# Last layer norm by halves, the last image placed by one-hot matmuls, bias rows spread by TensorE, row stores issued before weight fetches

## The reference, cut to what matters

```
h = tokenizer(x)                          # 8 images, 1024 tokens each, 256 wide
h = h + attention_layer(layernorm(h))     # 8 heads of 32
xf = layernorm(h)                         # "norm 3" of the kernel
H = gelu(xf @ W1 + b1)                    # 1024 wide
probs = softmax(H @ Wg + bg); assign = argmax(probs)      # 8 experts
y[token] = probs[token, assign] * (H[token] @ Wd[assign] + bd[assign])
out = h + y
```

## Time and profile before

| | |
|---|---|
| three runs | 1769.88, 1770.01, 1778.05 us, median 1770.01 |
| the profiled execution | 1766.45 us; its span from first to last instruction 1764.5 us |
| mean granted TensorE clock | 0.971 of full speed |
| busy share of the span | PE 91%, DVE 67%, ACT 53%, POOL 21% |
| last score of image 7 ends (PE) | 1403.96 us |
| first gather of rows is issued | 1483.89 us |
| second tile's turns begin; from here PE does a tile in 3.75 us | 1491.80 us |

### The profile page before, as it was taken

One profiled execution on the slowest core, in us unless ns is written; L12 is line 12 of the kernel. 1 busy time (PEld: TensorE's weight loads), 2 busy tenths in 40 slices (PEclk: granted clock), 3 DMA queues, 4 the chain that ended last, 5 costly groups with the idle time before them and its releaser, 6 DMA issues.

```text
span 1764.5 us, 29438 instructions
## 1 busy us (share of the span) xinstructions
PE 1610.8 (91%) x10934; PEld 1102.2 (62%) x10934; DVE 1185.5 (67%) x2070; ACT 940.5 (53%) x1564; POOL 369.2 (21%) x290
## 2 busy tenths in 40 slices
PE   8696999999999999999999999999888774999998
PEld 6463566555656565666466646664544363999998
DVE  2377777768686768677767776777765654555655
ACT  0364756665575657565756575658564751222222
POOL 0202000201120112012001301120110282555554
PEclk9898999999999999999999999999998986999999
DMA  4313044423533362436143604370429336566664
GB/s 172 88 47 81 13 120 96 109 50 92 118 77 84 65 139 49 111 49 135 42 114 55 154 15 114 58 164 2 96 61 215 72 85 163 189 211 212 212 201 143
DMA packets 131014, 188.57 MB, mean 107 GB/s; under 512 B 21606, under 2 KB 95980, under 8 KB 130620
## 3 DMA queue, kind: packets, MB, share of 16 engines
q1 hardware_dynamic: 112588, 121.57, 31.4%
q0 software_dynamic: 17856, 63.80, 11.2%
q10 hardware_dynamic: 432, 1.31, 0.2%
HBM read 85.55 MB, written 51.68 MB: 78 GB/s over the span
## 4 chain that ended last, share of the span: by engine, by line
PE 69%; DVE 11%; issue 8%; DMA 6%; ACT 4%; SPq 1%; POOL 1%; POOLq 0%; ACTq 0%; DVEq 0%
PE ps L576 12%; PE ps L827 12%; PE ps L590 11%; PE ps L543 8%; DVE nmax L1252 6%; PE ps L815 4%; PE ps L627 3%; PE ps L603 3%; PE ps L564 3%; ACT pr L953 3%; PE ps L610 3%; PE ps L649 3%; PE ps L651 2%; PE ps L650 2%; DMA xt<-x_in 2%
## 5 line engine op out<-in xcount | busy, mean ns | idle before, releaser
L1252 DVE TENSOR_REDUCE nmax<-ps 128x1 f32<-128x1024 f32 x512 | 623.6, 1221 | 220.9 <-PE ps L576 215.0
L953 ACT ACTIVATE pr<-ps,nmax 128x1024 f32<-128x1024 f32 x512 | 570.5, 1114 | 301.1 <-DVE nmax L1252 282.0
L576 PE MATMUL ps<-st 96*128 96x512 f32 x1024 | 400.5, 475 | 73.6 <-ACT pr L953 64.5
L576 PEld LDWEIGHTS ps<-st 96*128 96x128 f32 x1024 | 168.6, 192 | 270.7 <-ACT pr L953 133.4
L590 PE MATMUL ps<-pr,vs 128*32 128x256 f32 x4096 | 273.0, 387 | 10.9 <-DVE vs L1051 10.5
L827 PE MATMUL ps<-wd_high,hg 128*128 x1136 | 221.9, 288 | 0.0
L590 PEld LDWEIGHTS ps<-pr,vs 128*32 128x32 f32 x4096 | 109.3, 109 | 154.1 <-issue 73.7
L981 ACT ACTIVATE hg<-ps 128x512 fp32r<-128x512 f32 x142 | 77.4, 596 | 211.1 <-PE ps L815 211.1
L827 PEld LDWEIGHTS ps<-wd_high,hg 128*128 128x128 f32 x1136 | 182.1, 192 | 0.0
L543 PE MATMUL ps<-wp,xt 128*128 128x256 f32 x672 | 173.4, 379 | 3.4 <-DMA xt<-x_in 3.4
L827 PE MATMUL ps<-wd_low,hg 128*128 x568 | 160.8, 283 | 0.0
(11 more groups left out here) (153 smaller groups left out, 1938.8 us busy)
## 6 DMA issues: line engine op xcount, KB each, us to landing
st<-qk SPq DMA_DIRECT2D x192, 256.0 KB, 5.1
xt<-x_in SPq DMA_DIRECT2D x58, 384.0 KB, 4.1
token_rows<-staged_b SPq DMA_DIRECT2D x64, 256.0 KB, 4.9
token_rows<-staged_a SPq DMA_DIRECT2D x64, 256.0 KB, 4.9
token_rows<-hres POOLq DMA_DIRECT2D x8, 1024.0 KB, 5.4
wd_low<-w_down SPq DMA_DIRECT2D x64, 128.0 KB, 4.3
pr<-x_in SPq DMA_DIRECT2D x6, 384.0 KB, 10.0
rows<-token_rows,slot_from POOLq DMA_INDIRECT x71, 4.8
```

What stands on the lines that cost most here:

```text
L576: last = mm(ps[:, 2 * (k % SR) + j, :], stq[:, hh, i * P:(i + 1) * P], stk[:, hh, j * 512:(j + 1) * 512], start=True, stop=True)
L953: actv(pr[:, k % PR, :], ps[:, 2 * (k % SR):2 * (k % SR) + 2, :].rearrange("p a n -> p (a n)"), ACT.Exp, bias=nmax[:, k % 16:k % 16 + 1], ...
L1252: V.reduce_max(nmax[:, k % 16:k % 16 + 1], ps[:, 2 * (k % SR):2 * (k % SR) + 2, :].rearrange("p a n -> p (a n)"), AX_X, negate=True).then_ ...
```

## The change

1. SP: in image 7 the four `store_hidden` of image 6 are issued first, then `col`, then the weight pieces 0 to 14.
2. Norm 3 of the last image is done by halves on DVE and POOL (two `root_3`), and PE, ACT and DVE turn and split the first half alone; PE starts the hidden layer on it, and turns the second half after hidden chunk 2. POOL does 4 instead of 6 `split_down` before the first `root_3`.
3. The first half of the last image is no longer scattered: it is made one-hot like the second. Its 4 POOL scatters go, and 4 more one-hot matmuls (8 PE instructions as the profile counts them) come. `prefix` of the first half moves from after chunk 5 to after chunk 7; part of its `row_hot` is made between the copy and the sum of the logits; operations 8 and 9 of `route` (they give `prob`, which SP stores) move ahead of the count. POOL fetches `tab` before it waits for the stores of hidden rows.
4. `bd`, the bias row of each expert on all 128 partitions, was one broadcast DMA of 1 MB; now SP fetches 8 KB (`bd_raw`) in the place of `col`, ACT makes a selection matrix (`pick_row`), PE spreads the rows by 8 matmuls into four banks, and ACT copies them out.
5. The slots' experts (`slot_f`, `slot_expert`) are computed after `slot_from` and `slot_to`.

```diff
 (SP)
                 if before:
                     for u in range(4):
                         store_hidden(b - 1, u)
-                        if not after:
-                            for m in range(2 * u, 2 * u + 2):
-                                load_down(m)
                     if not after:
-                        for m in range(8, WD_PIECES - 1):
+                        sp.wait_ge(S["emb_mm"], IMAGES * TILES)
+                        sp.dma_start(col, column).then_inc(S["col_in"], 16)
+                        for m in range(WD_PIECES - 1):
                             load_down(m)
...
             sp.wait_ge(S["lg_done"], 2 * IMAGES)
-            sp.dma_start(col, column).then_inc(S["col_in"], 16)
+            sp.dma_start(bd_raw, b_down).then_inc(S["bd_raw_in"], 16)
             store_prob(IMAGES - 1)
-            sp.wait_ge(S["ff_mm"], 16 * IMAGES)
-            sp.dma_start(bd[:], b_down[None, :, :].broadcast_to([P, EXPERTS, D])).then_inc(S["bd_in"], 16)
...
 (POOL)
-            for m in range(6):
+            for m in range(4):
                 split_down(m)
-            root_3(IMAGES - 1)
+            for hf in range(2):
+                root_3(IMAGES - 1 + hf, slice(4 * hf, 4 * hf + 4))
+
+            pool.wait_ge(wd_in[2], 2 * 16 * (P // BLK))
             store_rear(IMAGES - 1, (IMAGES - 1) % 2)
             pool.wait_ge(S["xn_ready"], 2 * IMAGES)
-            for m in range(6, WD_PIECES):
+            for m in range(4, WD_PIECES):
                 split_down(m)
-            place(IMAGES - 1, IMAGES - 1, range(TILES // 2), IMAGES * STEPS - 4 * TILES)
             pool.wait_ge(S["row_ready"], 1)
             pool.wait_ge(S["lg_done"], 2 * IMAGES)
+            pool.wait_ge(S["table_out"], 16 * (ALL_TILES - TILES))
+            nc.gpsimd.indirect_dma_start(tab, None, table, bass.IndirectOffsetOnAxis(row_i[0:SLOTS, 0:1], 0)
+                                         ).then_inc(S["tab_in"], 16)
             for i in range(STAGED):
                 pool.wait_ge(row_out[i], 16 * IMAGES * 8)
-            pool.wait_ge(S["table_out"], 16 * (ALL_TILES - TILES // 2))
-            nc.gpsimd.indirect_dma_start(tab, None, table, bass.IndirectOffsetOnAxis(row_i[0:SLOTS, 0:1], 0)
-                                         ).then_inc(S["tab_in"], 16)
...
 (PE, router and end)
                     if k == 0:
-                        wait(pe, "xt_read", b * 4 + 4)
+                        wait(pe, "xt_read", b * 4 + (4 if b < IMAGES - 1 else 2))
                     if k >= 2:
                         wait(pe, "ff_act", b * 16 + k - 1)
                     hidden(b, 0, k, k)
+                    if b == IMAGES - 1 and k == 2:
+                        norm_turn(b, IMAGES * STEPS, (1,))
                 partial_logits(b, 0, 0)
+                wait(pe, "xt_read", b * 4 + 4)
...
-                    if b == IMAGES - 1 and k == HALF_PREFIX:
+                    if b == IMAGES - 1 and k == HC - 1:
                         prefix(b, ps[:, 0, :])
...
             prefix(IMAGES, ps[:, 1, :])
+            pe.wait_ge(S["bd_raw_in"], 16)
+            pe.wait_ge(S["sel_ready"], 1)
+            for e in range(EXPERTS):
+                last = mm(ps[:, 4 + e // 2, (e % 2) * D:(e % 2 + 1) * D], pick_row[:, e, :], bd_raw, start=True, stop=True,
+                          skip_group_check=True)
+                if e % 2 == 1:
+                    last.then_inc(S["bd_mm"], 1)
             pe.wait_ge(S["tab_in"], 16)
             mm(ps[:, 2, 0:SLOTS], tab, ident[0:SLOTS, 0:SLOTS], start=True, stop=False)
             pe.wait_ge(S["hot_ready"], 1)
-            for t in range(TILES // 2):
-                last = mm(ps[:, 2, 0:SLOTS], row_hot[:, t, :], slot_hot[:, t, :], start=False, stop=(t == TILES // 2 - 1))
+            for t in range(TILES):
+                last = mm(ps[:, 2, 0:SLOTS], row_hot[:, t, :], slot_hot[:, t, :], start=False, stop=(t == TILES - 1))
             last.then_inc(S["tab_mm"], 1)
+            pe.wait_ge(S["bd_in"], EXPERTS // 2)
...
 (ACT)
+            act.wait_ge(S["lg_done"], 2 * IMAGES)
+            actv(pick_row, ident[0:EXPERTS, 0:EXPERTS, None].broadcast_to([EXPERTS, EXPERTS, P]), ACT.Identity
+                 ).then_inc(S["sel_ready"], 1)
+            for i in range(EXPERTS // 2):
+                act.wait_ge(S["bd_mm"], i + 1)
+                actv(bd[:, 2 * i:2 * i + 2, :].rearrange("p e d -> p (e d)"), ps[:, 4 + i, :], ACT.Identity).then_inc(S["bd_in"], 1)
...
 (DVE)
+            def hot_rows(hf):
+                linked()
+                dve.wait_ge(S["col_in"], 16)
+                for t in range(4 * hf, 4 * hf + 4):
+                    at_tile = ALL_TILES - TILES + t
+                    last = V.tensor_scalar(row_hot[:, t, :], col, place_f[:, 0, t:t + 1], tid[:, at_tile:at_tile + 1],
+                                           ALU.is_equal, ALU.mult)
+                link(last)
...
                 logit_sums(last_b, hf)
+                if hf == 1:
+                    hot_rows(0)
                 keep_logits(last_b, hf)
...
-            for i in (0, 1, 2, 3, 4, 5, 6, 10):
+            for i in (0, 1, 2, 3, 4, 5, 6, 8, 9, 10):
                 route(last + 1, i)
```

More of the change, by code:

```diff
@@ L161, in vit_layer_kernel @@
         lt = xt_flat[:, 0:HALF]
+        row_hot = xt_flat[:, HALF:HALF + TILES * P].rearrange("p (t n) -> p t n", t=TILES)
+        col = row_hot[:, TILES - 1, :]
         staged = (staged_b, staged_a)
@@ L183, in vit_layer_kernel @@
         row_i = tensor(sc, "row_i", [P, 1], I32)
[L184 to L188 removed]
+        bd_raw = rows[0:EXPERTS, RING - 2, TILES * SLOTS:TILES * SLOTS + D]
+        pick_row = rows[0:EXPERTS, RING - 1, P:P + EXPERTS * P].rearrange("e (f n) -> e f n", f=EXPERTS)
+        slot_hot = rows[:, RING - 2, 0:TILES * SLOTS].rearrange("p (t n) -> p t n", t=TILES)
         sc.close()
@@ L442, in image @@
                 if before:
-                    root_3(b - 1)
+                    root_3(b - 1, slice(0, TILES))
                 if before:
@@ L629, in final, with norm_turn @@
                     last.then_inc(S["fin_mm"], 1)
-            def norm_turn(b, exps):
-                for j in range(4):
+            def norm_turn(b, exps, halves=(0, 1)):
+                for j in range(2 * halves[0], 2 * halves[-1] + 2):
                     hf, c = j // 2, j % 2
@@ L1004, in stats, with aggregate @@
                 aggregate(b, ln)
-            def aggregate(b, ln):
+            def aggregate(b, ln, tiles=range(TILES)):
                 hold(dve, f"stats{ln}", b + 1)
-                for t in range(TILES):
+                for t in tiles:
                     last = V.bn_aggr(mv[:, ln - 1, t, :], bst[:, ln - 1, t, :])
@@ L1088, in norm_3, with low_norm @@
                     last.then_inc(S["xn_ready"], 1)
-            def low_norm(b):
-                for j in range(4):
+            def low_norm(b, pieces):
+                for j in pieces:
                     piece = slice((j // 2) * HALF, (j // 2 + 1) * HALF)
@@ L1277, in _ @@
             added(last_b, last_par)
-            for t in range(TILES):
-                norm_3(last_b, last_par, t)
-            low_norm(last_b)
+            for hf in range(2):
+                for t in range(4 * hf, 4 * hf + 4):
+                    norm_3(last_b, last_par, t)
+                if hf == 0:
+                    low_norm(last_b, (0, 1))
             for hf in range(2):
@@ L1327, in _ @@
             linked()
-            link(V.tensor_tensor(pos[:, half], pos[:, half], cnt[:, 6, None, :].broadcast_to(each), ALU.add))
+            for hf in range(2):
+                link(V.tensor_tensor(pos[:, 4 * hf:4 * hf + 4], oh_half[:, (last + hf) % 2, GUARD:GUARD + TILES // 2, :],
+                                     cnt[:, 6, None, :].broadcast_to(each), ALU.mult))
             linked()
-            link(V.tensor_tensor(pos[:, half], pos[:, half], oh_half[:, IMAGES % 2, GUARD:GUARD + TILES // 2, :], ALU.mult))
+            link(V.reduce_sum(addr_f[:], pos[:], AX_X))
```

99 lines of the change are left out of this document (51 added, 48 removed).

## The result

| | before | after |
|---|---|---|
| median of 4 runs on one chip | 1771.13 us (1769.88 to 1778.05) | 1760.20 us (1757.43 to 1763.22) |
| ratio, with its 95% interval | | 0.993 [0.9907, 0.9953] |
| profiled execution (its span) | 1766.45 (1764.5) | 1760.89 (1759.1) |

The medians are 10.9 us apart. The same two kernels on another chip, later: 1767.92 (13 runs) and 1758.90 (8), ratio 0.995 [0.9932, 0.9967], 9.0 us. The forecast was 13.0.

What follows compares the result with a forecast made beforehand. PE, busy 91%, was taken to bound the kernel, with gains only where it waits: image 7's stores and the tail. 5.3 + 8.2 - 0.5 = 13.0 us off 1766.45 gives 1753.5, or 1757.0 against the runs' median; range 1752 to 1766.

Steps and rivals of the forecast that it cites:

- the likeliest case: Whole kernel: the forecast itself, 13.0 us off, 1757.0 against the runs' median; chance 72%.
- Part 1: Image 7, hidden-row stores issued before weights: ACT's third exponential 5.3 us sooner, bounds 3.7 to 5.3.
- Rival (b): Image 7: the earlier stores give nothing, leaving 7.7 us gained, 1762.3; chance 9%.
- Part 2: Last image's norm by halves: first half's hidden layer starts 4.2 us sooner, net 2.3 after turns and clock.
- -0.9 for the turns, -1.0 for the clock: Last hidden layer: losses set against the 4.2 us, for 8 turns moved between hidden chunks and for full speed returning differently.
- Part 3a: Tail: first prefix moved into PE's wait for the last Gelu, net 0.65 us gained.
- Part 3b: Tail without scatters: POOL fetches `tab` straight after `row_ready`, so it is there at 1470.6 instead of 1480.8.
- same moment: Tail: `hot_ready` from DVE at 1470.6, just when `tab` is there.
- Part 4: Tail, bias rows: `bd_raw` lands at 1466, matmuls end 1472.1, first gather at 1475.7, 8.2 us sooner.
- the slow bound: Tail: the 8 bias matmuls wholly at half clock, 7.2 us; 3.6 at full clock, 6.1 taken.
- Rival (a): Tail: `bd_raw` lands like `column`, 12.0 us after issue, so the tail gains nothing; 4.4 us off, 1765.6; chance 15%.
- Rival (c): Last hidden layer: PE stays at half clock, 19 us lost against 13 gained, 1776; chance 4%.

Runs made afterwards that it cites:

- part 1 alone: Kernel before with all 15 weight pieces issued behind the four hidden-row stores: 1761.66 us, ratio 0.9959 (second chip); 1761.00 us, 0.9960 (third chip).
- the norm in one piece: Changed kernel with the last norm whole again, four weight splits ahead of it kept: 1761.74 us, ratio 0.9965 (second chip); 1760.33 us, 0.9954 (third chip).
- the second trace: Trace of the changed kernel, nothing altered, run again on the third chip: 1758.90 us (8 runs), ratio 0.9950 to the kernel before.
- b_split_4: Kernel before with 4 instead of 6 POOL weight splits ahead of the norm, two more behind it: 1770.67 us, ratio 1.0015.
- the kernel of 1754.85 us: Changed kernel with fifth split before the norm, later routing, bias matmuls halved around the table, slots' experts ahead of the `tab_mm` wait: 1754.85 us, 0.9930.

## Why the prediction was right, and where not

The time was as forecast within 3.2 us and inside the range, and the likeliest case is the one that came. Its steps fared differently, and the total is nearer than they are. On the third chip part 1 alone gave 6.9 us for 5.3, and all the rest 2.1 for 7.7. That most of the forecast gain came all the same is in part luck.

**Part 1, right.** 5.4 us for 5.3, shown by undoing it and by doing it alone. What was not in it is the clock behind the stall, at half in the first 6 us in all three traces that have the stall. From the third exponential to the final projection the two first traces differ by 0.9 us, the trace where part 1 was undone by 8.9; how much of either is the stall's was not measured. Rival (b) did not occur: ACT's wait before the third exponential is 1.02 us, for DVE.

**Part 2, the start right, the net too large.** The first hidden matmul came 5.3 us sooner for 4.2 (turns at full clock, 1.12 us; POOL's power 1.05 for 1.67). The term "-0.9 for the turns, -1.0 for the clock" was mis-sized. What the runs showed in place of the net 2.3 is 0.8 us against the norm in one piece, by the trace, and 1.4 by medians that don't tell the two apart. The missing piece is a sentence of the prediction: that POOL's splits end later "and nobody needs them before 1480". Nobody needs their result, but DVE needs to run beside them. Its small operations with both inputs in SBUF were held until a split ended, 1.96, 2.44 and 1.82 us for 0.19, 0.18 and 0.15. This delayed `run`, PE waited for it, and the last logits ran at half clock. Whether DVE gets in between two splits or not matters little: the last held operation ended with the last split in either case (1452.43 and 1452.39 here, 1446.70 and 1446.65 in the second trace). That the hold goes with the splits is shown in both directions: two pieces more behind the norm brought it into the kernel before, and two less took one hold and 2.3 us away. The last logits' clock goes with the wait for `run`. Ten traces have the changed tail; in the five where PE waited 1.48 to 2.43 us for `run` the last logits took 2.81 to 3.47 us, in the five where it waited 0.85 us or not at all they took 1.92. So the price of the holds in the changed kernel's first trace is about 3.3 us, 1.77 of wait and 1.5 of clock.

The Trainium skill has the rule, in "SBUF — State Buffer", section "Who interferes with whom": a VectorE instruction with two inputs in SBUF contends with a GpSimd instruction that reads SBUF, and the one that was first blocks the other for its whole length. The traces agree, 12 splits of 2.355 us and holds that end on their ends. They show more than the rule says, too. DVE did not always get in when a split had ended: it stood through two ends in two traces (6.55 us each) and through one in two others (2.73 us in `b_split_4`, 3.19 with the norm in one piece). And the norm, whose operations have one tensor as input, was slowed beside a split (1.88 and 2.66 us for 1.37). Block turns between the held operations kept their time (0.70 us at 1449.98).

**Part 3a**, the prefix, lies in the stretch that the holds cover; its 0.65 us can't be seen by itself.

**Part 3b, right.** Without scatters the fetch of `tab` follows `row_i` at once (0.48 us), `tab` was there at about 1468.6 (the fetch starts at 1465.93 and lands 2.6 us later in the profile's list of DMAs), and DVE's table was ready at 1469.74: the "same moment" of the prediction.

**Part 4, mis-sized in four terms of 0.6 to 1.2 us.** The path was as described, from the last logits to the first gather, but it took 17.98 us and not 14.4 (19.65 before). `bd_raw` landed 5.5 us behind the last logits for 4.7, since SP was in the last stores until 1462.04; they had been issued late, for the block turns stood behind the held operations. The bias matmuls took 7.19, not 6.1: the clock did not return within them, and 7.2 was the slow bound. The one-hots took 4.1, not 2.9, for the same reason. The first gather started 1.24 us behind `slot_from`, not 0.65; every kernel with the changed tail shows 1.24 or 1.25 and every one without it 0.65, and taking work off DVE between `slot_from` and the gather, in the kernel of 1754.85 us, did not change it. Its cause stays open. That the bias rows were on the path with nothing gained from standing there is shown by the run that put them last: 3.4 us.

**Rival (a), right in its mechanism.** With scatters `b_down` lands 11.7 us behind its issue, in the way of `column`'s 12.0; without them 3.6. The Trainium skill's rule on strongly ordered writes, as the prediction quotes it from "DMA: Bandwidth & Descriptors", section "Queues, rings and completion order", agrees with this: only scatters on another queue were added, and `b_down` landed at 1471.19, half a microsecond behind the last of them (POOL's wait for them ended at 1470.72). Which writes it stood behind no trace shows. **Rival (c)** did not occur in the hidden layer (0.92 in the window from its first matmul to the first prefix), and in the tail PE was granted 0.58, where the earlier trace rows have 0.50 for the kernel before: the bias and one-hot matmuls were at half clock, as the slow bounds had them:

```profile
1422.81:1454.34 31.53, 28.98 (x129) 21.80 (x129) 18.90 (x30) 16.89 (x24) 28.26 (x12) 0.92 0.44 100
1454.34:1482.00 27.66, 17.37 (x66) 12.06 (x66) 15.34 (x69) 3.84 (x7) 3.94 (x4) 0.58 0.46 99
```

Taken together, part 1 gave about 7 us by the medians and parts 2 to 4 about 2, a gain that is not told from none (1758.90 for 1761.00 with part 1 alone, third chip; the intervals overlap; from the final projection to the first gather the traces have 71.40 and 71.55 us with part 1 alone, and 69.04 and 72.00 for the changed kernel, the latter with 2.0 us lost in a final projection at half clock). The forecast had 5.3 and 7.7.

## What to carry to other kernels

A helper engine's long background work costs nothing only if nobody on the path runs small operations beside it: before moving it, lay its start and end over the timeline of VectorE and mark the operations with two SBUF inputs; here the norm, with one, was slowed as well. What stands ahead of a step on the path has a limit too: one split too many before `root_3` cost about 1.1 us in three traces. Work that fills an idle stretch of PE belongs behind the thing that the path waits for, or cut to what the wait holds; here 3.4 us went because eight matmuls stood in front of a table that had come. And a stall on PE is to be priced with the half clock right behind it, which is part of what its removal brings.

## What the runs showed of the hardware

- A VectorE operation of 128x32, 0.19 us alone, took up to 6.55 us beside GpSimd operations of 128x1024 of 2.36 us, and its end fell on the end of one of them within 0.05 us. In four traces that was not the first end that it met.
- Four VectorE TENSOR_SCALAR operations of 128x256, 1.37 us without a GpSimd operation beside them, took 1.88 and 2.66 us beside one of 2.37 us.
- Four scatters of 4-byte elements on GpSimd's queue made an 8 KB load on SP's queue land 11.7 us after its issue instead of 3.6. The 64 KB of `column` landed 11.3 to 12.0 us after their issue in the four traces that load it beside such scatters, and 4.1 to 5.3 in the ten that load it in image 7.
- 16 matmul instructions of 8 rows and 256 columns, 7.19 us without a pause, left PE at half clock to their end, in all eight traces that have them together.
- After the stall in image 7 PE's mean clock up to the final projection was 0.74, 0.89 and 0.92 in three executions (67.28, 59.23 and 57.42 us): what followed one and the same wait differed by nearly 10 us. Without the stall it was 0.88 to 1.00 (54.16 to 58.72 us).
- Executions that are alike up to image 7 reach it up to 6.4 us apart, so two single spans can't be subtracted where a few microseconds matter.
